# A conditional adapter and mixture kernel: b2 through one-hot rows, root and reciprocal for the norm, first units by pairs, front reordered

## What is computed

```python
# layer 0: one of 10 adapters per sequence, rank 32
h       = relu(x @ W1[lang] + b1[lang])
y       = x + h @ W2[lang] + b2[lang]
normed  = (y - mean(y)) * rsqrt(var(y) + 1e-5)
x1      = x + normed * gamma[lang] + beta[lang]
# layer 1: three shared MLPs (128 -> 512 -> 128), two of four experts
s_m     = relu(x1 @ share_wi[m]) @ share_wo[m]           # m = 0, 1, 2
e       = wa * expert[type](x1) + wb * expert[type + 1](x1)
g       = softmax(relu(concat(e, s_0, s_1, s_2)[token 0] @ gate_w1) @ gate_w2)
out     = x1 + g0 * e + g1 * s_0 + g2 * s_1 + g3 * s_2
```

## Time and profile before

| what | value |
|---|---|
| runs of the kernel before | 87.37 us median of 3 (87.27 to 89.02) |
| the profiled execution's own time | 86.99 us |
| its span in the trace | 85.2 us |
| mean granted PE clock | 0.995 of full |
| busy: PE / PEld / DVE / ACT / POOL | 79.8 / 66.4 / 62.4 / 49.8 / 39.9 us |

### The profile page before, as it was taken

The page is one execution under the profiler, slowest core; times in us unless marked ns, Lnnn a source line. Parts: engine busy times, 40 slices in busy tenths (PEclk is TensorE's granted clock), DMA queues, the critical chain, the costliest instruction groups (busy, mean ns, idle before and its releaser), DMA issues.

```text
span 85.2 us, 1653 instructions
## 1 busy us (share of the span) xinstructions
PE 79.8 (94%) x472; PEld 66.4 (78%) x472; DVE 62.4 (73%) x175; ACT 49.8 (58%) x117; POOL 39.9 (47%) x79
## 2 busy tenths in 40 slices
PE   4999999989999999999999899999999999999950
PEld 1376767856888888888999688888999898999820
DVE  4338788999799765456389985459777999389970
ACT  6001195992896599586799364464627555376410
POOL 5950191887339149998667400000001995029800
PEclk9999999999999999999999999999999999999997
DMA  0566755999998294000000000000000000210004
GB/s 1 134 153 135 191 125 151 338 239 358 333 307 268 29 345 133 0 0 8 0 0 0 0 0 0 0 0 0 0 8 0 4 0 0 65 47 23 0 0 123
DMA packets 11998, 7.49 MB, mean 88 GB/s; under 512 B 2358, under 2 KB 10836, under 8 KB 11988
## 3 DMA queue, kind: packets, MB, share of 16 engines
q1 hardware_dynamic: 10784, 6.76, 27.8%
q10 hardware_dynamic: 1076, 0.59, 2.8%
q0 software_dynamic: 128, 0.02, 0.2%
HBM read 5.80 MB, written 0.52 MB: 74 GB/s over the span
## 4 chain that ended last, share of the span: by engine, by line
PE 64%; DVE 14%; issue 7%; POOL 7%; ACT 4%; DVEq 0%; ACTq 0%
PE bank L982 9%; PE bank L962 8%; PE bank L979 8%; PE bank L980 7%; PE bank L963 7%; PE bank L966 7%; PE bank L1013 4%; DVE hl L756 4%; POOL prod L488 3%; PE bank L919 2%; PE bank L913 2%; PE bank L1007 2%; PE bank L987 2%; ACT hh L553 2%; POOL prod L490 2%
## 5 line engine op out<-in xcount | busy, mean ns | idle before, releaser
L756 DVE SCALAR_TENSOR_TENSOR hl<-bank,hh 128x256 fp32r<-128x256 f32 (+2 forms) x60 | 31.4, 526 | 12.4 <-ACT hh L553 11.9
L553 ACT ACTIVATE hh<-bank 128x256 fp32r<-128x256 f32 (+2 forms) x60 | 28.0, 468 | 15.5 <-PE bank L966 14.9
L456 POOL TENSOR_TENSOR wl<-w_raw,wh 128x512 fp32r<-128x512 f32 x17 | 21.7, 1292 | 8.1 <-ACT wh L546 8.1
L982 PE MATMUL bank<-hl,wh 128*128 128x256 f32 (+2 forms) x60 | 20.7, 345 | 0.8 <-DVE hl L756 0.7
L979 PE MATMUL bank<-hh,wh 128*128 128x256 f32 (+2 forms) x60 | 19.8, 330 | 0.0
L980 PE MATMUL bank<-hh,wl 128*128 128x256 f32 (+2 forms) x60 | 19.6, 326 | 0.0
L982 PEld LDWEIGHTS bank<-hl,wh 128*128 128x128 f32 x60 | 11.3, 189 | 3.8 <-DVE hl L756 2.9
L962 PE MATMUL bank<-x1hl,wh 128*128 128x256 f32 (+1 forms) x36 | 12.2, 338 | 0.0
L979 PEld LDWEIGHTS bank<-hh,wh 128*128 128x128 f32 x60 | 11.4, 190 | 0.8
L980 PEld LDWEIGHTS bank<-hh,wl 128*128 128x128 f32 x60 | 11.4, 189 | 0.7
L966 PE MATMUL bank<-x1hl,wh 128*128 128x256 f32 (+1 forms) x36 | 11.5, 319 | 0.0
(11 more groups left out here) (111 smaller groups left out, 108.9 us busy)
## 6 DMA issues: line engine op xcount, KB each, us to landing
w_raw<-in_L_cond_expert_wi_dram SPq DMA_DIRECT2D x6, 256.0 KB, 3.9
w_raw<-in_L_cond_expert_wo_dram SPq DMA_DIRECT2D x6, 256.0 KB, 4.2
x_in<-in_x_dram SPq DMA_DIRECT2D x2, 256.0 KB, 3.4
w_raw<-in_L_cond_share_wi_dram SPq DMA_DIRECT2D x2, 256.0 KB, 3.9
w_raw<-in_L_cond_share_wo_dram SPq DMA_DIRECT2D x2, 256.0 KB, 4.1
xs<-x1hl SPq DMA_DIRECT2D x4, 128.0 KB, 4.4
x1hl<-xs SPq DMA_DIRECT2D x4, 128.0 KB, 2.7
out_dram<-o_sb SPq DMA_DIRECT2D x4, 128.0 KB, 1.9
```

The costliest lines, as they stand in the source:

```text
L456: nc.gpsimd.tensor_tensor(wl[:, k, w, :], w_raw[:, k, buf(w), :], wh[:, k, w, :].bitcast(f32), ALU.subtract).then_inc(s_wl[w], 1)
L553: nc.scalar.activation(packed(hh[:, u % NBUF, :], r), packed(h_ps[u % NBUF][:, :], r), ACT.Relu).then_inc(s_hh, 1)
L756: nc.vector.scalar_tensor_tensor(out=packed(hl[:, u % NBUF, :], r), in0=packed(h_ps[u % NBUF][:, :], r), scalar=0.0, in1=packed(hh[:, u % ...
L982: nc.tensor.matmul(dst, wh[:, 1, w, chunk], lo, start=False, stop=(c == FC - 1)).then_inc(s_mm2, 1)
```

## The change

The diff, cut to its core (indented four columns less):

- **b2.** `W2z` and `ha` now have one block per pair. Rows 0 to 63 hold the two sequences' adapters; rows 64 to 127 of `ha` hold one-hot rows (written once by DVE, two copies), and `W2z` holds b2 there (two DMAs from POOL with b2 repeated over the pairs). `residual_bias` is gone: `adapter_out` adds b2. `adapter_relu` becomes two instructions of 64 rows per half.
- **Norm.** `ve` and POOL's power are gone. ACT takes the root of variance + epsilon (`standard_deviation`), DVE the reciprocal. ACT's first table is the one of Sqrt instead of Exp.
- **Moves.** `add_beta` goes from ACT to POOL, `weights_low(1, 0)` from DVE to POOL. On PE the gamma and beta columns come before `adapter_in(0)`, and `transpose_x(1)` before `adapter_out(0)`. On DVE the copy of these columns comes before the statistics.
- **First units.** `opening_products` makes the first products of units 0 and 1 pair by pair, 256 columns at a time.

```diff
...
-    W2z = sb("W2z", [P, NH, HB, D])
+    W2z = sb("W2z", [P, PAIRS, PAIR, D])
...
-    ha = sb("ha", [P, NH, S])
+    ha = sb("ha", [P, PAIRS, S])
...
         engine.wait_ge(s_zero, 1)
         for j, lang in zip(js, langs):
-            engine.dma_start(W2z[A * j:A * j + A, h, j, :],
+            n, i = divmod(h * HB + j, PAIR)
+            engine.dma_start(W2z[A * i:A * i + A, n, i, :],
                              W2[bass.ds(lang, 1), :, :].rearrange("l a d -> (l a) d")).then_inc(s_w2[h], 16)
     def load_wi(engine, w, src):
...
-        nc.gpsimd.iota(lang_no[:, :], pattern=[[0, 1]], base=0, channel_multiplier=1,
-                       allow_small_or_imprecise_dtypes=True).then_inc(s_langno, 1)
+        for k in range(P // A):
+            nc.gpsimd.iota(lang_no[A * k:A * k + A, :], pattern=[[0, 1]], base=0, channel_multiplier=1,
+                           allow_small_or_imprecise_dtypes=True).then_inc(s_langno, 1)
+        pool.wait_ge(s_langno, P // A)
...
-        pool.dma_start(par_l[:, 0, :], b2).then_inc(s_par, 16)
-        pool.dma_start(par_l[:, 1, :], gamma).then_inc(s_gb, 16)
-        pool.dma_start(par_l[:, 2, :], beta).then_inc(s_gb, 16)
+        pool.dma_start(par_l[:, 0, :], gamma).then_inc(s_gb, 16)
+        pool.dma_start(par_l[:, 1, :], beta).then_inc(s_gb, 16)
+        pool.wait_ge(s_zero, 1)
+        for i in range(PAIR):
+            k = A * (PAIR + i)
+            pool.dma_start(W2z[k:k + L, :, i, :], b2.rearrange("l (n d) -> l n d", n=1)
+                           .to_broadcast([L, PAIRS, D])).then_inc(s_par, 16)
         pool.dma_start(gv[:, :, :].rearrange("p t e -> p (t e)"),
                        gate_vecs.rearrange("(o t) e -> o (t e)", o=1).to_broadcast([P, T * E])).then_inc(s_gv, 16)
-        link(nc.gpsimd.memset(minus_half[:, :], -0.5))
+        nc.gpsimd.memset(eps[:, :], EPS).then_inc(s_eps, 1)
...
-        def inverse_deviation(n):
-            pool.wait_ge(s_ve, n + 1)
-            b = slice(n * PAIR, (n + 1) * PAIR)
-            nc.gpsimd.tensor_tensor(rstd[:, b], ve[:, b], minus_half[:, :], ALU.pow).then_inc(s_rstd, 1)
+        def add_beta(h):
+            pool.wait_ge(s_colsc, 1)
+            pool.wait_ge(s_xtc[h], 1)
+            for b in range(h * HB, (h + 1) * HB):
+                nc.gpsimd.tensor_scalar(xT_beta[:, seq(b)], xT[:, seq(b)], cols_c[:, 1, b:b + 1], None,
+                                        ALU.add).then_inc(s_xb, 1)
...
-        inverse_deviation(0)
-        inverse_deviation(1)
+        add_beta(0)
         weights_low(0, (0,))
         weights_low(0, (1,))
-        inverse_deviation(2)
-        inverse_deviation(3)
-        weights_low(1, (1,))
+        add_beta(1)
+        weights_low(1)
...
-        nc.scalar.activation(one[:, 1:2], one[:, 0:1], ACT.Exp)
+        nc.scalar.activation(one[:, 1:2], one[:, 0:1], ACT.Sqrt)
...
-        def add_beta(h, js=range(HB)):
-            act.wait_ge(s_colsc, 1)
-            if h == 0:
-                act.wait_ge(s_xtc[0], 1)
-            for b in (h * HB + j for j in js):
-                nc.scalar.activation(xT_beta[:, seq(b)], xT[:, seq(b)], ACT.Identity,
-                                     bias=cols_c[:, 1, b:b + 1]).then_inc(s_xb, 1)
+        def standard_deviation(n):
+            act.wait_ge(s_eps, 1)
+            act.wait_ge(s_mv, PAIR * (n + 1))
+            b = slice(n * PAIR, (n + 1) * PAIR)
+            nc.scalar.activation(deviation[:, b], mv[:, b, 1], ACT.Sqrt, bias=eps[:, :]).then_inc(s_dev, 1)
...
-            nc.scalar.activation(ha[:, h, :], w1_ps[:, seq(h)], ACT.Relu, bias=b1_c[:, h:h + 1]).then_inc(s_h0a, 1)
+            for n in (2 * h, 2 * h + 1):
+                nc.scalar.activation(ha[0:PAIR * A, n, :], w1_ps[0:PAIR * A, seq(n)], ACT.Relu,
+                                     bias=b1_c[:, n:n + 1]).then_inc(s_h0a, 1)
...
         adapter_relu(0)
+        act.wait_ge(s_xt, 2)
+        nc.scalar.activation(xT[:, cols(1)], xt_ps[1][:, :], ACT.Copy).then_inc(s_xtc[1], 1)
         act.wait_ge(s_tab, 1)
         table = loaded(act, "table", tab_i[0:1, HB:place(SLOTS, 0)],
                        [B - 1] * HB + [B - size(k) for k in range(SLOTS)])
         ranks, starts = dict(zip(range(HB, B), table)), table[HB:]
-        act.wait_ge(s_xt, 2)
-        nc.scalar.activation(xT[:, cols(1)], xt_ps[1][:, :], ACT.Copy).then_inc(s_xtc[1], 1)
+        standard_deviation(0)
         weights_high(0, 0)
-        add_beta(0)
+        standard_deviation(1)
         adapter_relu(1)
+        weights_high(0, 1)
         x1_high(0)
         x1_high(1)
-        weights_high(0, 1)
-        act.wait_ge(s_xtc[1], 1)
-        add_beta(1)
+        standard_deviation(2)
+        standard_deviation(3)
...
-        link(nc.vector.tensor_copy(lang_f[:, :], lang_p[0:L, :]))
-        dve.wait_ge(s_langno, 1)
+        link(nc.vector.tensor_copy(lang_f[:, :], lang_p[:, :]))
+        dve.wait_ge(s_langno, P // A)
         nc.vector.tensor_scalar(onehot[:, :], lang_f[:, :], lang_no[:, :], None, ALU.is_equal).then_inc(s_onehot, 1)
+        dve.wait_ge(s_onehot, 1)
+        for i in range(PAIR):
+            rows = slice(A * (PAIR + i), A * (PAIR + i) + A)
+            nc.vector.tensor_copy(ha[rows, :, :], onehot[rows, i:B:PAIR].unsqueeze(2)
+                                  .to_broadcast([A, PAIRS, S])).then_inc(s_hot, 1)
...
-            dve.wait_ge(s_mv, PAIR * (n + 1))
-            b = slice(n * PAIR, (n + 1) * PAIR)
-            nc.vector.tensor_scalar(ve[:, b], mv[:, b, 1], EPS, None, ALU.add).then_inc(s_ve, 1)
         def norm_apply(n):
+            dve.wait_ge(s_dev, n + 1)
+            both = slice(n * PAIR, (n + 1) * PAIR)
+            nc.vector.reciprocal(rstd[:, both], deviation[:, both]).then_inc(s_rstd, 1)
             dve.wait_ge(s_rstd, n + 1)
             for b in range(n * PAIR, (n + 1) * PAIR):
                 dve.wait_ge(s_mv, b + 1)
...
-        nc.vector.tensor_copy(b1_c[:, :], b1_ps[:, 0:NH]).then_inc(s_b1c, 1)
+        nc.vector.tensor_copy(b1_c[:, :], b1_ps[0:PAIR * A, 0:PAIRS]).then_inc(s_b1c, 1)
         sort_by_type()
         window_tables()
+        dve.wait_ge(s_cols, 1)
+        nc.vector.tensor_copy(cols_c[:, :, :].rearrange("p n b -> p (n b)"), cols_ps[:, 0:2 * B]).then_inc(s_colsc, 1)
         norm_stats(0)
         norm_stats(1)
-        dve.wait_ge(s_cols, 1)
-        nc.vector.tensor_copy(cols_c[:, :, :].rearrange("p n b -> p (n b)"), cols_ps[:, 0:2 * B]).then_inc(s_colsc, 1)
...
-            if u == 0:
-                weights_low(1, 0)
             if u in (0, 1):
                 norm_apply(u + 2)
             if u in (2, 3):
...
-                pe.wait_ge(s_h0a, h)
+                pe.wait_ge(s_h0a, PAIR)
             for j in range(HB):
-                mm = nc.tensor.matmul(w1_ps[A * j:A * j + A, seq(h)], W1s[:, h * HB + j, :], xT[:, seq(h * HB + j)],
+                n, i = divmod(h * HB + j, PAIR)
+                mm = nc.tensor.matmul(w1_ps[A * i:A * i + A, seq(n)], W1s[:, h * HB + j, :], xT[:, seq(h * HB + j)],
...
-        def residual_bias(n):
-            for i in range(PAIR):
-                b = n * PAIR + i
-                nc.tensor.matmul(y_ps[n][:, seq(i)], onehot[:, b:b + 1].to_broadcast([L, P]), par_l[:, 0, :],
-                                 start=False, stop=False, skip_group_check=True)
         def adapter_out(h):
             pe.wait_ge(s_w2[h], 16 * HB)
-            pe.wait_ge(s_h0a, h + 1)
-            for k in range(2):
-                nc.tensor.matmul(y_ps[2 * h + k][:, pair(0)], ha[:, h, :], W2z[:, h, k * PAIR:(k + 1) * PAIR, :],
+            if h == 0:
+                pe.wait_ge(s_par, 16 * PAIR)
+                pe.wait_ge(s_hot, PAIR)
+            for n in (2 * h, 2 * h + 1):
+                pe.wait_ge(s_h0a, n + 1)
+                nc.tensor.matmul(y_ps[n][:, pair(0)], ha[:, n, :], W2z[:, n, :, :],
                                  start=False, stop=True, skip_group_check=True).then_inc(s_y, 1)
...
-            if u == 0:
-                pe.wait_ge(s_x1h, PAIRS // 2)
...
+        def opening_products():
+            w = set_of(0)
+            pe.wait_ge(s_wh[w], 1)
+            pe.wait_ge(s_wl[w], 1)
+            for n in range(PAIRS // 2):
+                pe.wait_ge(s_x1h, n + 1)
+                for u in range(AHEAD):
+                    dst, chunk = h_ps[u][:, pair(n)], slice(u * P, (u + 1) * P)
+                    high = x1hl[:, n * PAIR:(n + 1) * PAIR, 0, :]
+                    nc.tensor.matmul(dst, wh[:, 0, w, chunk], high, start=True, stop=False, skip_group_check=True)
+                    nc.tensor.matmul(dst, wl[:, 0, w, chunk], high, start=False, stop=False, skip_group_check=True)
+                pe.wait_ge(s_x1l, n + 1)
+                for u in range(AHEAD):
+                    mm = nc.tensor.matmul(h_ps[u][:, pair(n)], wh[:, 0, w, u * P:(u + 1) * P],
+                                          x1hl[:, n * PAIR:(n + 1) * PAIR, 1, :], start=False, stop=True,
+                                          skip_group_check=True)
```

(52 more changed lines are left out.)

2 lines of the change are left out of this document (removed).

## The result

The changed kernel takes 87.69 us (median of 20 runs, 86.76 to 88.59), the kernel before 87.22 us beside it (20 runs, 87.00 to 89.02). The ratio leaves out the few executions that ran over 1.5% above their kernel's fastest (three and two), while the medians of all alone would give 1.0054. The single times say more than the median: four of the 20 lie at 86.76 to 87.12, the other 16 at 87.64 or above, with nothing between (of e1's seven, one lies between, at 87.24). The profiled execution, 86.89 us with a span of 85.1, is one of the four. So I profiled the same kernel once more (e1) and caught one of the 16.

The account below looks back on a forecast made before the run. PE, busy 94% of the span, bounds the kernel, so only its waits count. Unit 1's 0.6 gain, all else hidden, gives 86.99 - 0.6 = 86.4 profiled and 87.37 - 0.6 = 86.8 median; range 86.0 to 88.3.

Parts of the forecast that it names:

- What the gain meets next: Unit 2 to first slot product: product moves from 26.00 to 25.4, only xs's landing caps the gain, the 0.6 passes.
- rival A: Exp's table load on ACT shows and PE waits in unit 9: 1.0 lost, 0.6 won, 87.8 us; chance 0.15.
- Rival B: DVE's reciprocals are held by POOL as `ve` was: 87.5 if only the first, 89.3 if all; chance 0.12.
- Statistics of pair 0: DVE's start of the first pair's statistics in the front: 9.47, with bounds 9.2 and 9.9.
- The norm: Front, statistics to z: two reciprocals replace work on DVE's list, root 0 hidden (at worst 0.25 late), z ends at 12.65.
- The opening: PE's first products of units 0 and 1 pair by pair, finished at about 15.4: buys nothing by itself.
- The new wait: Roots 2 and 3 ahead of hidden_high(0) on ACT: hidden values 0 start at 16.3; gain at first L982 0.2.
- Unit 1: DVE's hl of unit 1 starts at 18.40; PE's second L982 moves from 19.70 to 19.1, a gain of 0.6.
- POOL's additions for beta: Eight additions moved to POOL, taken at 0.4 each (bounds 0.13 and 0.46), 1.6 per half: hidden.
- The cap of xs: Last xs copy lands at 24.98, unchanged, before the first slot product: caps the front's gain at 1.0.
- C: Rival: the front wins nothing, root 0 late by 0.25, only the subtraction's move off DVE gains: 87.2; chance 0.18.
- D: Rival: statistics start at 9.2 and relus are quick, the gain reaches xs's cap of 1.0: 86.4; chance 0.10.

Follow-up runs that it names:

- e5: Changed kernel with DVE's x1_low(2) and x1_low(3) both after hidden_low(4) instead of hidden_low(5); 87.01 us, ratio 0.9982.
- e6: Changed kernel with the move of e5, and POOL's sequence_weights one subtraction later (behind slot 2's first weights); 86.28 us, ratio 0.9891.
- e9: Kernel before the change with both moves of e6 (x1_low at unit 4, sequence_weights one subtraction later); 86.83 us, ratio 0.9966.
- e12: e8 with adapter_out(0) ahead of transpose_x(1) on PE again, as in the kernel before; 86.84 us, ratio 0.9941.
- e10: e8 with the pair-by-pair opening taken back, the first products of units 0 and 1 one after the other; 85.98 us, ratio 0.9857.
- e8: e6 with the roots of pairs 2 and 3 moved behind hidden_high(0) in ACT's list; 85.76 us, ratio 0.9834.
- e11: e8 with the subtraction weights_low(1, 0) back on DVE behind hidden_low(0); 86.59 us, ratio 0.9935.
- e4: Changed kernel without b2's two DMAs on POOL's queue and PE's wait for them (b2 left out of the sum); 87.44 us, ratio 1.002.

## Why the prediction was wrong

**The step that failed** stands under "What the gain meets next": only xs's landing was looked at as a cap, and from it "The 0.6 passes under it" and the sum 86.99 - 0.6. Two other things stand on the way from there to the end: DVE's low parts of half 1 beside POOL's subtraction, 0.16 us apart in the kernel before, and POOL's list at unit 16. A lead moves each engine's list by another amount (0.48 and 0.29 here), so that margin was the number to read. e5 against the changed kernel gives the collision's price, 0.7 us of the median; e6 against e5 the price of POOL's list, 0.7; and e6 against e9 the front's real gain, 0.55 (medians taken on different chips, on which the kernel before differs by 0.06 at most). Of the second, one part stays open: why POOL starts its list late in the changed kernel. The measured 87.69 lies beside rival A's 87.8 by chance, since nothing of A happened, and even the lower group misses the forecast (86.89 in the profiled execution, 86.4 said), since the list takes most of the lead.

**Rival B had the mechanism and named the wrong instructions.** It looked among one-input instructions, for which `ve` and the gate vectors stood in the rows, and I left out two-input ones on SBUF, though DVE has six of them, two on x1hl and four on xs, near POOL's work. The first of those on x1hl was held as well, which the forecast had at nothing. It takes 0.41 undisturbed. In e5 it took 1.01, behind POOL's second subtraction for set 0 (timeline, then the view of the line, in ns):

```profile
13.03 1.29 POOL L469 TENSOR_TENSOR wl<-w_raw,wh 128x512 fp32r<-128x512 f32 x1 [0.48 <-ACT wh L557]
```

```profile
L762 DVE TENSOR_TENSOR x1hl<-x1T,x1hl x2: 413/712/1010, 13.6 to 14.5; 128x256 fp32r<-128x256 f32 x2
```

It took 0.77 in e1 and 0.47 at 86.89, where it started later (13.73 and 13.92). In the kernel before, POOL's second subtraction began at 15.08, behind both; the change has ACT round those weights earlier (12.12 instead of 14.39). An earlier front loses lead here: in e5 the first low part began 0.33 sooner than at 86.89, and the second ended no sooner (14.94 and 14.91). The reciprocals were never held: 0.16 at 11.94, inside POOL's 11.61 to 14.11. What tells the ones that are held from the others is not the size: beside a POOL subtraction bn_aggr and the reciprocal weren't held, `ve` (tensor_scalar) was, a two-input subtraction was.

**Statistics of pair 0**, 9.47 said, 9.90 and 9.71 measured, inside the bounds: PE's transposes ended at 8.89 rather than 8.77, and 0.28 went by in waiting for W2. **The one-hot copies**, at most 1.4, took 0.87 and were hidden. **The norm**: from statistics to z 1.40, my sum 1.5; right. The ten registers were hidden too, as said, but "at worst 0.25" was far off: in e12 0.73 pass between copy and root, with no other work of ACT's there. PE's new order, booked as a loss of 0.1, is what hides them, and is worth 1.1 of the whole (e12).

**The opening** buys nothing: right (e10). **The new wait** in ACT's list: hidden values 0 right behind root 3 at 16.42, as forecast to 0.1. But I read from it only that a gain of 0.2 was left. That the wait itself was what bound the next stretch, and cost 0.5 of the whole, is what e8 shows. **Unit 1**: 0.6 said, 0.42 and 0.49 measured; hl and reciprocal came as worked out, each 0.1 to 0.2 late. Taking the subtraction off DVE is the term that carries it (e11: 0.8 of the whole).

**POOL's additions for beta** took 0.60 each (2.36 for half 0; 2.51 for half 1, where the first took 0.77 beside DVE's low part), above both of my bounds. They held up no x1T: it wanted the first at 12.78, they ended at 10.97. **The cap of xs** is not fixed at 24.98. The last copy lands at 24.4 in e8 (PE's product at 25.09), at 25.1 in the execution at 86.89, but at 26.1 in e6's profiled one (the product at 26.43), where it took 5.5 us instead of 4.8. In the changed kernel at 86.89 and in e8 it didn't bind; in e6's it came 0.3 ahead of PE's product, and whether it bound there was not tried.

**Rival A, the table switch,** didn't come true. ACT in the profile at 86.89:

```profile
26.58 1.28 ACT L595 ACT_TABLE_LOAD   x1
28.12 0.21 ACT L595 ACTIVATE gq<-gq 128x12 f32<-128x12 f32 x1 [0.25 <-DVE gq L708]
```

The load began 0.02 behind the end of the hidden values of unit 8 (26.18 + 0.38 = 26.56), took 1.28 and left 0.25 over, as forecast to 0.02. In e1 nothing was left over (load 27.60, Exp 28.89), yet PE had no gap there. C is false (the front did win 0.4 to 0.5 at unit 1), and D's gain of 1.0 in the front showed in none of the two traces.

**Still open**: why POOL's L476 starts 0.50 us after the end of the reciprocal that releases it in the changed kernel (29.96 + 0.18 = 30.14 to 30.64; e1 and e5 likewise) and 0.16 in the kernel before and in e4. That is as large as the difference between 0.47 of lead at unit 8 and 0.11 at unit 16. e4 differs by two DMAs fewer on POOL's queue (and PE's wait for them) and has the old gap, 0.14, so they have to do with it, or the place of L476 in a list that is shorter by them; which of the two, and by what way it acts 25 us later, was not tried.
